# Eight x tiles with a semaphore each, in a graph kernel whose row parts shared a semaphore with x

## The reference

```
def adjacent_mat(adj):
    adj = adj + eye
    deg = sum(adj, axis=1)
    dinv = where(deg > 0, deg ** -0.5, 0)
    return dinv[:, None] * adj * dinv[None, :]

adj = adjacent_mat((A + A.T) * 0.5)
y = A @ adj
y = y @ x
out = layernorm(x + y, axis=-1)
```

## Time and profile before

| what | value |
|---|---|
| median of three runs | 440.7 us (439.79 to 441.95) |
| the profiled execution's own time | 440.35 us |
| its span, first to last instruction | 438.4 us |
| busy: PE / PEld / DVE / ACT / POOL | 392.4 / 316.9 / 284.1 / 142.5 / 113.1 us |
| mean granted clock of PE | 0.959 of full |
| chain that ended last | issue 50%, DMA 18%, DVE 11%, SP 9%, PE 5%, POOL 3%, ACT 2% |
| transfers of x tiles in that chain | 4% of the span |
| data moved | 81.98 MB, mean 187 GB/s |

### The profile page before, as it was taken

One profiled execution on the slowest core, in us unless ns is written; L12 is line 12 of the kernel. 1 busy time (PEld: TensorE's weight loads), 2 busy tenths in 40 slices (PEclk: granted clock), 3 DMA queues, 4 the chain that ended last, 5 costly groups with the idle time before them and its releaser, 6 DMA issues.

```text
span 438.4 us, 5717 instructions
## 1 busy us (share of the span) xinstructions
PE 392.4 (90%) x1724; PEld 316.9 (72%) x1724; DVE 284.1 (65%) x508; ACT 142.5 (33%) x256; POOL 113.1 (26%) x153
## 2 busy tenths in 40 slices
PE   5497899947979859989999999999999999999994
PEld 4375787835847737867777788888888888888883
DVE  1898486536894665567777765766666666666642
ACT  3566467424921321122222231222222222222210
POOL 2669587424892000122222000000000000000000
PEclk9699699979899988999999999999999999999999
DMA  8969999993448999999999587555555555555500
GB/s 279 385 199 290 305 286 268 241 235 79 122 108 189 224 228 230 235 222 224 225 224 223 128 189 212 150 145 147 145 147 144 144 144 144 146 142 147 139 24 24
DMA packets 71967, 81.98 MB, mean 187 GB/s; under 512 B 5776, under 2 KB 44048, under 8 KB 71952
## 3 DMA queue, kind: packets, MB, share of 16 engines
q1 hardware_dynamic: 71952, 81.81, 75.0%
HBM read 65.01 MB, written 4.19 MB: 158 GB/s over the span
## 4 chain that ended last, share of the span: by engine, by line
issue 50%; DMA 18%; DVE 11%; SPq 9%; PE 5%; POOL 3%; ACT 2%; POOLq 0%; DVEq 0%; ACTq 0%
DMA rows<-adj 9%; DMA x_slots<-x 4%; DVE w_lo L791 3%; SPq L298 3%; DMA u_raw<-un 3%; DVE rows L796 2%; DVE cols L759 2%; SPq L314 2%; SPq L309 2%; PE ps L512 2%; DMA cols<-adj 2%; SPq L318 2%; DMA z<-z_raw 1%; POOL rstd L480 1%; POOL cols L447 1%
## 5 line engine op out<-in xcount | busy, mean ns | idle before, releaser
L491 PE MATMUL ps<-z,w_lo 128*128 128x512 f32 x256 | 99.6, 389 | 0.0
L490 PE MATMUL ps<-z,w_hi 128*128 128x512 f32 x256 | 99.6, 389 | 0.0
L489 PE MATMUL ps<-z,w_hi 128*128 128x512 f32 x256 | 99.6, 389 | 0.0
L489 PE MATMUL ps<-u_hi,w_hi 128*128 128x512 f32 x176 | 71.6, 407 | 14.2 <-DVE w_lo L791 11.3
L791 DVE TENSOR_TENSOR w_lo<-cols,w_hi 128x512 fp32r<-128x512 f32 x112 | 80.2, 732 | 5.3 <-ACT w_hi L653 1.4
L744 ACT ACTIVATE w_hi<-cols 128x512 fp32r<-128x512 f32 x64 | 39.8, 633 | 128.0 <-DVE cols L796 128.0
L490 PE MATMUL ps<-u_lo,w_hi 128*128 128x512 f32 x176 | 69.7, 396 | 0.0
L491 PE MATMUL ps<-u_hi,w_lo 128*128 128x512 f32 x176 | 69.5, 395 | 0.0
L480 POOL TENSOR_TENSOR rstd<-var_eps,mhalf 128x1 f32<-128x1 f32 x16 | 8.8, 548 | 187.7 <-DVE var_eps L959 187.7
L491 PEld LDWEIGHTS ps<-z,w_lo 128*128 128x128 f32 x256 | 48.1, 188 | 10.1
L489 PEld LDWEIGHTS ps<-z,w_hi 128*128 128x128 f32 x256 | 48.0, 188 | 10.0
(11 more groups left out here) (71 smaller groups left out, 455.6 us busy)
## 6 DMA issues: line engine op xcount, KB each, us to landing
rows<-adj SPq DMA_DIRECT2D x108, 256.0 KB, 5.0
cols<-adj SPq DMA_DIRECT2D x44, 256.0 KB, 6.4
z<-z_raw SPq DMA_DIRECT2D x64, 128.0 KB, 5.5
x_slots<-x SPq DMA_DIRECT2D x16, 256.0 KB, 7.8
u_raw<-un SPq DMA_DIRECT2D x64, 64.0 KB, 4.5
x_res<-x SPq DMA_DIRECT2D x16, 256.0 KB, 2.6
out<-y_out SPq DMA_DIRECT2D x16, 256.0 KB, 2.1
rows<-adj SPq DMA_DIRECT2D x3, 512.0 KB, 4.9
```

Source lines behind the costliest of these rows:

```text
L489: nc.tensor.matmul(out_, hi, mov_hi, start=first, stop=False)
L490: nc.tensor.matmul(out_, hi, mov_lo, start=False, stop=False)
L491: return nc.tensor.matmul(out_, lo, mov_hi, start=False, stop=last)
```

## The change

There are eight slots for x tiles in place of four. The row part and the x tile of a step now have semaphores of their own: four for row parts, one for each x slot. PE and DVE wait for the row part alone; ACT waits for its x tile at line 689 of every step. The x load of step k waits for step k - 8, where it waited for step k - 4, so that the loads of steps 4 to 7 wait for nothing. The order of the instructions is the same on every engine.

The four added tiles take 8 KB of each partition. The place for them comes from a region at the bottom of the memory that the program leaves free: it is cut from 16 KB to 1 KB, and all tiles move down. Nothing else uses the added tiles.

```
+    XS = 8
-        place = [16640]
+        place = [1152]
...
-        x_in = [x_slots[h][:, n] for h in range(2) for n in range(2)]
+        x_more, _ = sb("x_more", [P, XS - 4, D], F32)
+        x_in = [x_slots[h][:, n] for h in range(2) for n in range(2)] + [x_more[:, n] for n in range(XS - 4)]
...
-        s_rx = [sem(f"row_and_x_loaded{s}") for s in range(4)]
+        s_rp = [sem(f"row_part_loaded{s}") for s in range(4)]
+        s_x = [sem(f"x_loaded{s}") for s in range(XS)]
...
-        s_x0 = sem("x0_loaded")
...
-        def row_x_count(k):
-
-            return 32 * (k // 4 + (k % 4 > 0))
+        def x_count(k):
+            return 16 * (k // XS + 1)
+
+        def row_count(k):
+            return 16 * (k // 4 + (k % 4 > 0))
...
                 sp.dma_start(piece(0, k, k, NB).rearrange("p b c -> p (b c)"),
-                             a_rows[k, :, k * P:N]).then_inc(s_rx[k % 4], 16)
+                             a_rows[k, :, k * P:N]).then_inc(s_rp[k % 4], 16)
...
-                if k >= 4:
-                    sp.wait_ge(s_ul, k - 3)
-                    sp.wait_ge(s_un, k - 3)
-                sp.dma_start(x_in[k % 4], x_rows[k]).then_inc(s_rx[k % 4], 16)
+                if k >= XS:
+                    sp.wait_ge(s_ul, k - XS + 1)
+                    sp.wait_ge(s_un, k - XS + 1)
+                sp.dma_start(x_in[k % XS], x_rows[k]).then_inc(s_x[k % XS], 16)
...
                 elif b0 == k:
-                    pe.wait_ge(s_rx[k % 4], row_x_count(k))
+                    pe.wait_ge(s_rp[k % 4], row_count(k))
...
-                if k == 0:
-                    act.wait_ge(s_x0, 16)
+                act.wait_ge(s_x[k % XS], x_count(k))
                 act.wait_ge(s_dinv, k + 1)
...
                 if k >= 1:
-                    dve.wait_ge(s_rx[k % 4], row_x_count(k))
+                    dve.wait_ge(s_rp[k % 4], row_count(k))
...
-    nc = bacc.Bacc("TRN2", target_bir_lowering=False, num_devices=1)
+    nc = bacc.Bacc("TRN2", target_bir_lowering=False, num_devices=1, dynamic_dma_scratch_size=1024)
```

More of the change, by code:

```diff
@@ L268, in load_first @@
                     sp.dma_start(piece(1, 0, b, HALF * h + HALF), a_cols[0, :, b:HALF * h + HALF]).then_inc(s_c0[h], 16)
-                sp.dma_start(x_in[0], x_rows[0]).then_inc(s_x0, 16)
+                sp.dma_start(x_in[0], x_rows[0]).then_inc(s_x[0], 16)
             def load_step(k):
@@ L688, in _ @@
                     act.wait_ge(s_used, k - 2)
-                nc.scalar.activation(un_hi[:, k % 3], x_in[k % 4], ACT.Copy, scale=dinv[:, k:k + 1]).then_inc(s_uh, 1)
+                nc.scalar.activation(un_hi[:, k % 3], x_in[k % XS], ACT.Copy, scale=dinv[:, k:k + 1]).then_inc(s_uh, 1)
                 if k >= 2:
                     act.wait_ge(s_ustrip[k % 2], 64 * (k // 2))
-                nc.scalar.activation(un[:, k % 2], x_in[k % 4], ACT.Copy, scale=dinv[:, k:k + 1]).then_inc(s_un, 1)
+                nc.scalar.activation(un[:, k % 2], x_in[k % XS], ACT.Copy, scale=dinv[:, k:k + 1]).then_inc(s_un, 1)
                 u_high_strips(*U_AFTER.get(k, (0, 0)))
@@ L784, in u_low @@
                 dve.wait_ge(s_uh, k + 1)
-                nc.vector.scalar_tensor_tensor(un_lo[:, k % 3], x_in[k % 4], dinv[:, k:k + 1], un_hi[:, k % 3],
+                nc.vector.scalar_tensor_tensor(un_lo[:, k % 3], x_in[k % XS], dinv[:, k:k + 1], un_hi[:, k % 3],
                                                ALU.mult, ALU.subtract).then_inc(s_ul, 1)
@@ L853, in _ @@
                 if k == 1:
-                    dve.wait_ge(s_x0, 16)
+                    dve.wait_ge(s_x[0], 16)
                     u_low(0)
```

## The result

The changed kernel takes **446.7 us** as the median of four runs (444.22 to 449.02), the kernel before beside it 440.25 us (438.82 to 441.95): a ratio of 1.015, 95% interval 1.0102 to 1.0198. Ratios and intervals here are of executions in the kernel's fast state alone and can differ by up to 0.3% from the quotient of the medians. The forecast was 439.7 us, 0.2% less than before, with a range up to 441.9. The changed kernel is slower by 1.5%, an outcome to which the forecast gave a chance of 0.08.

The account below looks back on a forecast made before the run. In the first 100 us PE waits for data, SP for u, and transfers are never far from full. Terms 0 + 0 + 0.65 + 0.3, about 1.0 us less: 439.7 us against the median of 440.7, range 438.0 to 441.9.

Parts of the forecast that it names:

- The memory moved: 0: Tiles and bottom region: addresses change, sizes don't, and nothing here uses the cut descriptor ring; worth 0.
- Step 5: PE starts when the column part lands, at 43.94 (gain 1.34 us), idle 1.51 us, clock kept; gain not passed on.
- SP 1.1 us earlier at 54.82: SP's strip copy at 54.82 waited for u of step 5; SP can be 1.1 us earlier.
- The looser wait of the x load: x load on SP: its waits ended no idle time, four slots were enough, no transfer issued earlier; worth 0.
- No new wait for x at line 689: ACT's added wait is already met, since line 689 waits for dinv anyway; worth 0.
- The rival of the falling clock: PE idle 1.55 us before step 9, clock falls, step costs up to 3.6 us more: 443.6 us; chance 0.1.
- Step 9: PE starts at 66.66, after the column part's landing at 66.60, where it was 67.31: gain 0.65 us.
- a transfer that is issued earlier into a full queue does not land earlier: Loads before step 9, DMA share 1.04: the reason to take 0.65 us there, not 1.75.
- The 358 GB/s: HBM rate for one core; against 295 GB/s it left a sixth unused, which would make the sum 1.75 us.
- reach the strips: Next stage's strips, at 77.81, start 0.65 us earlier, plus 0.3 for room in the queue on the way.
- gain of 0.65 to 1.0 us: Whole kernel: 0.65 us from step 9, about 1.0 us with the 0.3 added for queue room.
- The rival on the region: The cut region serves SP's transfers after all, each issue stretches by 0.6 us: 500 us; chance 0.03.

Follow-up runs that it names:

- e1: Kernel before with all its tiles moved up by 128 bytes (start 16768, not 16640), nothing else: 447.43 us, ratio 1.0168.
- e2: Changed kernel with its tiles 128 bytes higher, from 1280, a multiple of 256: 439.64 us, ratio 0.9986.
- e5: Changed kernel with its tiles starting at 1536, a multiple of 512: 439.24 us, ratio 0.9977.
- e12: Changed kernel with its tiles starting at 2048: 439.2 us, ratio 0.998.
- e13: Changed kernel with tiles from 1280, only the tiles that columns are loaded into moved 128 bytes off 256: 445.82 us, ratio 1.0138.
- e9: Changed kernel with tiles from 1280, the two row tiles alone moved 128 bytes off 256: 439.76 us, ratio 0.9989.
- e4: Changed kernel with four x slots, tiles and region as in the kernel before, so the semaphores alone: 439.38 us, ratio 0.9982.
- e10: Changed kernel with tiles from 1280, u alone moved 128 bytes off 256: 440.76 us, ratio 0.9983.
- e3: Kernel before with the bottom region cut to 1 KB and its tiles left where they were: 439.14 us, ratio 0.9995.
- e6: Changed kernel with its tiles starting at 1344, 64 bytes beyond a multiple of 256: 456.05 us, ratio 1.0342.
- e7: Changed kernel with its tiles starting at 1472, 192 bytes beyond a multiple of 256: 455.57 us, ratio 1.0362.
- e11: Changed kernel with tiles from 1280, z (with row and column tiles inside it) and x tiles 128 bytes off 256: 447.73 us, ratio 1.0165.
- e14: Changed kernel with tiles from 1280, the high and low matmul weights alone 128 bytes off 256: 444.81 us, ratio 1.0122.

## Why the prediction was wrong

**The step that failed is "The memory moved: 0".** It said "Addresses change, sizes don't" and looked only at what the region was for. The start of the tiles, read against 256, costs 1.5 to 1.7% (e1, and back again in e2); all other parts of the change together measure 0.1 to 0.2% faster, not clear of nothing (e2, e5, e12). No row of the kernel before could show the price, because all its tiles lay well; but the number in the diff could be divided by 256, and a bound belonged there, since the forecast itself had found the queue full: where transfers are the limit, a few per cent on each of them come out at the end.

A hint was to be had. The Trainium skill, "DMA: Bandwidth & Descriptors", section "How a descriptor splits into AXI transactions", says that each access has to start at a multiple of 256 bytes, so that a transfer piece that starts between two of them also pays for bytes that it doesn't use. It says this of reading, and here it is the written side that moved. The runs agree that 256 is the step (starts at 64, 128 and 192 lose, e2, e5 and e12 don't). They show further that 512-byte runs suffer (e13), while the row tiles do not measurably (e9). The Trainium skill's count of beats is not borne out: by that, as an estimate, a 512-byte run would cost 18 beats at 64, 20 at 128 and 22 at 192 where it costs 16 at 0; the packets of 6 to 33 us took 100.2, 101.3 and 100.9%, no different. The measurement decides.

**What else held.** Step 5: forecast at 43.94 with 1.51 us idle and the clock kept; 43.47, 1.38 us and kept, and in e4 43.82, 1.48 us and kept. SP 1.1 us earlier at 54.82: it was. The looser wait of the x load and the eight slots: nothing, e2 and e4 are alike. No new wait for x at line 689 shows: the 16 idle times there are 19.7 us together (13 of them, 13.1 us, have no releaser in the trace), 20.4 before. The rival of the falling clock did not come about; but to set 1.51 and 1.55 us between 1.29 and 2.09 was no ground for that, since the length of an idle time alone did not decide. In the kernel before, PE was idle for 2.19 us until 188.91 and kept a granted clock of 1.00, and in e10 for 2.46 us until 57.42.

**What did not hold, beside the memory.** Step 9 was forecast at 66.66 and started at 66.55, but that agreement is in part luck: its column part took 9.6 us, and with the tiles at a multiple of 256 it took 7.4 to 9.3 us and step 9 starts at 65.68 (e4), 63.37 (e2), 65.10 (e5) and 66.00 (e12). That "a transfer that is issued earlier into a full queue does not land earlier" did not come out in these runs: e4 issued the column part of step 9 at 56.55, 1.35 us earlier than before, and it landed at 65.55, 1.05 us earlier; in e2, e5 and e12 it landed 0.7 to 3.4 us earlier. The 358 GB/s that the prediction took from the Trainium skill is no bound in this trace either: from 10 to 20 us the kernel before moved 383 GB/s.

The gain was then to reach the strips, 0.65 us and 0.3 more. The strips start at 77.70 in e4, 77.48 in e5 and 77.87 in e12, against 77.81: ACT's u of step 9 waits there for the copies of an earlier u, 1.08, 0.89 and 0.83 us; the prediction has no term for that wait. Over the first 115 us ACT's waits for these copies are 16.5 us in the changed kernel and 12.6 in e4, 9.0 before. In e2 the strips do start early, at 74.79, but in e3, which has none of the semaphores, they start at 75.53, so single profiles can't tell what the semaphores gave there.

**The size of the gain** of 0.65 to 1.0 us can't be told from nothing by these runs. e2, e4, e5 and e12 all stand at 0.998 to 0.999, which is what was forecast, but each interval reaches 1, and e3, which has no such gain, stands at 0.9995; by medians e3 (439.14 us) is no slower than e2 and e4 (439.64 and 439.38), which ran beside it.

**The rival on the region** had its place right and its cause wrong: cutting the region is free (e3), what is done with the freed room is not.

## What to carry to other kernels

When a change moves tiles, take their new starts modulo 256 before anything else, above all for tiles that are loaded in short runs (of 512 bytes here); in this kernel 128 bytes cost 6 to 7 us of 440, where the rest of the change could bring about one. A diff that adds a buffer changes every address behind it: put the base at a multiple of 256, and compare the packets' time for the same megabytes in a stretch that the schedule can't have touched. If tiles are shifted, shift both operands of a matmul alike.

## What was not expected of the hardware

- Loads into tiles that start off a multiple of 256 bytes took 8 to 11% more packet time per megabyte from 6 to 33 us (e1, e6, e7, e13); later strip loads suffer more at 64 and 192 than at 128, and no run here shows why.
- Where weights and streamed operand lay 128 bytes apart, modulo 256, each 128 x 512 matmul started 2 to 3% later (e11: 233.3 ns, e14: 232.4 ns, otherwise 226.7 on z; e10: 232.4 ns against 227.2 on u), at the same granted clock of 1.00 and with PE busy throughout. Only a difference of 128 was tried, and no run shows the mechanism.
- PE kept its clock of 2.4 GHz (granted 1.00 from 43.4 to 72 us) through idle times of 1.38, 1.21, 1.33 and 1.29 us, and in e10 (granted 1.00 from 42 to 76 us) through 1.97, 1.87, 2.46 and 1.83 us.
